# The rows of x2 by target: fetched through the first layer's packed list and a table, and the attention layer in two column parts

## The reference

```
h = max(layernorm(x), 0);  x = x + L0(h, src, dst)        # sums over edges, 1/sqrt(1 + degree)
h = max(layernorm(x), 0);  x = x + L1(h, [src, dst])      # polynomial of the graph Laplacian, 4 steps
h = max(layernorm(x), 0);  x = x + L2(h, src, dst, type)  # attention over edges, 86 relation types
h = max(layernorm(x), 0);  x = x + L3(h, src, dst)        # 10 steps of propagation, summed at dst
```

## Time and profile before

| | |
|---|---|
| median of three runs | 2741.11 us (2739.32 to 2743.00) |
| the profiled execution | 2739.09 us, span 2737.3 us |
| POOL busy | 1796.4 us (66%), 1786 instructions |
| DVE busy | 1731.8 us (63%), 2937 instructions |
| PE busy | 430.9 us (16%) |
| ACT busy | 341.8 us (12%) |
| granted TensorE clock | 1.0 |

### The profile page before, as it was taken

How to read it: one execution, slowest core, us unless ns; L and a number is a source line. 1 busy time by engine, 2 the same in 40 slices (tenths; PEclk the granted TensorE clock), 3 DMA queues, 4 the chain that set the end, 5 groups by cost and what they waited for, 6 DMA issues and landing times.

```text
span 2737.3 us, 12492 instructions
## 1 busy us (share of the span) xinstructions
PE 430.9 (16%) x2105; PEld 214.0 (8%) x2105; DVE 1731.8 (63%) x2937; ACT 341.8 (12%) x1043; POOL 1796.4 (66%) x1786
## 2 busy tenths in 40 slices
PE   0000000000001000000000097293294000016000
PEld 0000000000001000000000032031131000016000
DVE  8998897987129978278996078487888820420000
ACT  0000022111000110011211043141142200000000
POOL 6566677777742473577777656756556777466776
DMA  1001022221000131112210100100000210000000
GB/s 20 15 10 26 14 61 51 51 68 32 12 7 4 62 129 25 33 47 86 51 34 14 10 2 6 10 2 6 6 7 8 87 40 10 29 11 10 8 8 8
DMA packets 68011, 76.87 MB, mean 28 GB/s; under 512 B 34800, under 2 KB 60873, under 8 KB 67193
## 3 DMA queue, kind: packets, MB, share of 16 engines
q0 software_dynamic: 56384, 23.45, 6.5%
q1 hardware_dynamic: 5720, 27.38, 2.6%
q10 hardware_dynamic: 5856, 25.60, 2.5%
HBM read 35.67 MB, written 46.87 MB: 30 GB/s over the span
## 4 chain that ended last, share of the span: by engine, by line
DVE 45%; issue 27%; POOL 11%; PE 7%; another core or an unknown queue 5%; DMA 2%; ACT 1%; DVEq 1%; ACTq 0%; SPq 0%; POOLq 0%
POOL out L1573 9%; DVE mf L521 4%; DVE psum L903 3%; DVE psum L918 3%; DVE z L521 3%; DVE pay L521 2%; DVE outs L521 2%; PE psum L2017 2%; DVE pay L904 2%; PE psum L2018 2%; POOL mf L1567 1%; DVE psum L550 1%; DVE psum L913 1%; DVE xs L908 1%
## 5 line engine op out<-in xcount | busy, mean ns | idle before, releaser
L1567 POOL DMA_INDIRECT xs<-in_x,i_src x196 | 200.8, 1025 | 134.4 <-issue 56.4
L1567 POOL DMA_INDIRECT xd<-x_rows,i_dstX x196 | 195.9, 1000 | 128.5 <-DVE z L1377 93.9
L1567 POOL DMA_INDIRECT xd<-in_x,i_dst x196 | 205.1, 1046 | 109.3 <-DVE mf L521 47.5
L1573 POOL DMA_INDIRECT out<-outs,i_outS x196 | 200.7, 1024 | 112.7 <-issue 41.4
L1567 POOL DMA_INDIRECT mf<-x_rows,i_srcX x196 | 207.5, 1059 | 72.1 <-issue 72.1
L1573 POOL DMA_INDIRECT out<-outs,i_srcX x196 | 196.7, 1003 | 69.3 <-issue 58.9
L1567 POOL DMA_INDIRECT pay<-payload_by_dst,i_rank x196 | 195.2, 996 | 62.9 <-issue 62.9
L521 DVE TENSOR_TENSOR pay<-psum,pay 128x512 f32<-128x512 f32 x196 | 132.4, 688 | 117.5 <-ACT pay L1895 59.5
L521 DVE TENSOR_TENSOR mf<-mf 128x128 f32<-128x128 f32 (+5 forms) x578 | 175.7, 342 | 10.4
L2017 PE MATMUL psum<-pay 64*128 64x512 f16 x196 | 117.6, 600 | 183.6 <-ACT pay L1880 96.3
L1377 DVE TENSOR_REDUCE z<-pay 128x512 f32 (+1 forms) x196 | 132.4, 676 | 0.0
(11 more groups left out here) (458 smaller groups left out, 2398.4 us busy)
## 6 DMA issues: line engine op xcount, KB each, us to landing
z<-in_x ACTq DMA_DIRECT2D x14, 624.0 KB
out<-z ACTq DMA_DIRECT2D x14, 624.0 KB
l_first_rows<-mf SPq DMA_DIRECT2D x2, 3234.0 KB
outs<-in_x ACTq DMA_DIRECT2D x6, 624.0 KB
out<-outs ACTq DMA_DIRECT2D x6, 624.0 KB
l_own_rows<-pay SPq DMA_DIRECT2D x1, 3626.0 KB, 11.1
payload_by_dst<-z SPq DMA_DIRECT2D x1, 3234.0 KB
x_rows<-z SPq DMA_DIRECT2D x1, 3234.0 KB
```

What stands on the lines that cost most here:

```text
L1567: G.indirect_dma_start(out=dest(k), out_offset=None, in_=table, in_offset=bass.IndirectOffsetOnAxis(ap=idx[:, k:k + 1], axis=0), bounds_ch ...
L1573: G.indirect_dma_start(out=table, out_offset=bass.IndirectOffsetOnAxis(ap=idx[:, k:k + 1], axis=0), in_=source(k), in_offset=None, bounds_ ...
```

## The change

The target rows are no longer gathered one set of 128 for each of 196 columns. What `xd` holds before (the closed form for every edge) is stored by SP as a table `y_dram` in edge order, behind the store of x2. The listing of L1 packs a third value, the rank of the edge in target order (`rank_f`), so that each of the 128 x 46 list slots also knows the row of its edge (`dst_slot`). After L1, POOL gathers x2 for the list slots by `pf0` (46 columns, `PACKED`), then the source rows of part 0 (76), then scatters `PACKED` into the table by `dst_slot` (46), and SP loads the whole table back into `xd`; DVE waits for both transfers (`y_table`, 32) inside `l2_inputs`. If a list were longer than XW, the Else branch gathers all 196 columns as before.

The attention columns go in two parts, 0 to 76 and 76 to 196. The source rows of part 1 are all gathered during the first 18 turns, 50 columns free and then one for each finished column, so the listing of L3 follows the first 18 turns, and then inputs 1 (120 columns) and 31 turns. The sends are 40 beside the listing, 20 free, 124 beside the last turns.

```diff
-L2_PARTS = ((0, 76), (76, 140), (140, EC))
+L2_PARTS = ((0, 76), (76, EC))
 XS_PARTS = ((0, 66), (66, 140), (140, 180), (180, EC))
 OWN_PARTS = ((0, 140), (140, 180), (180, EC))
-L2_TURNS = ((0, 18), (18, 34), (34, EC // 4))
-ROWS_FREE = (0, 60, 50)
-SENDS_LISTING, SENDS_FREE, SENDS_BESIDE = 40, 20, 56
+L2_TURNS = ((0, 18), (18, EC // 4))
+ROWS_FREE = 50
+SENDS_LISTING, SENDS_FREE, SENDS_BESIDE = 40, 20, 124
...
-        g_at = 2 * HOT_N + 2 * CELL_N
-        EDGES = {"l1": edge_groups(two(out_t, 0, HOT_N), two(out_t, 2 * HOT_N, CELL_N), two(out_t, g_at, GIVEN_N)),
+        GIVEN3_N = XG * W * 3
+        EDGES = {"l1": edge_groups(two(out_t, 0, HOT_N), two(out_t, 2 * HOT_N, CELL_N), two(z_t, 0, GIVEN3_N), 3),
-                                   [out_t[:, late:late + GIVEN_N], xs_t[:, late:late + GIVEN_N]])}
-        assert g_at + 2 * GIVEN_N <= EW and x4c_at + 2 * HOT_N <= EC * OWNW
+                                   [out_t[:, late:late + GIVEN_N], xs_t[:, late:late + GIVEN_N]], 2)}
+        rank_f = z_t[:, 2 * GIVEN3_N:2 * GIVEN3_N + EC]
+        both_f = z_t[:, 2 * GIVEN3_N + EC:2 * GIVEN3_N + EC + 6 * W]
+        PACKED = pay[:, x4c_at:x4c_at + W * X2W].rearrange("p (q w) -> p q w", w=X2W)
...
             sp.wait_ge(s["s2_ready"], 1)
             sp.dma_start(x2_dram.rearrange("(p c) w -> p (c w)", p=P), z_t[:]).then_inc(s["s2_stored"], 16)
+            by_dst = y_dram.rearrange("(p c) w -> p (c w)", p=P)
+            sp.dma_start(by_dst, xd_t[:]).then_inc(s["y_table"], 16)
             sp.wait_ge(s["fits1_set"], 1)
             longest = sp.value_load(fits[0:1, 0:1], min_val=0, max_val=EC)
...
+                sp.wait_ge(s["y_scattered"], 16 * W)
+                sp.dma_start(xd_t[:], by_dst).then_inc(s["y_table"], 16)
...
             def keyed(ids, w, idx, cont, head, carried, away):
 
-                empty = c["st2"][:, 0:2 * w].rearrange("p (q v) -> p q v", v=2)
+                nv = len(idx)
+                empty = c["st2"][:, 0:nv * w].rearrange("p (q v) -> p q v", v=nv)
                 link(ts(empty, ids, 0.5, FAR, ALU.is_lt, ALU.mult))
                 link.many([V.scalar_tensor_tensor(out=out, in0=ids[:, :, k], scalar=-1.0, in1=empty[:, :, k],
...
-            def compact_edges(ptr, own, turned, edges):
+            def compact_edges(given, pointers, turned, edges, both):
...
-                for value, out in zip((ptr, own), values):
+                for value, out in zip(given, values):
...
+                nv = len(given)
+                ids = c["sq_out"][:, 0:nv * W].rearrange("p (q v) -> p q v", v=nv)
+                gathered_up(ids, W, nv, both)
+                keyed(ids, W, pointers, contc, headc, wc[:], nohome)
...
+            link(V.tensor_copy(rank_f, icols["edgeS"][:]))
             link(V.tensor_copy(icols["l1"][:], PAY[:, :, D]))
-            compact_edges(PAY[:, :, D], col("send"), wt, EDGES["l1"])
+            compact_edges((PAY[:, :, D], col("send"), rank_f), (pf0, owni, dst_slot[:]), wt, EDGES["l1"], both_f)
             segment_sums(link, PAY[:, :, 0:D], s["carry_in"], s["carry_out"], 1, None)
             marks["summed"] = link.n
...
                 halves_of(xy16[:, :, 0:D], xy16[:, :, D:2 * D], xy[:, :, D:2 * D])
-                dve.wait_ge(s[f"x2dst_in{part}"], 16 * w)
+                dve.wait_ge(s["y_table"], 32)
                 layernorm(xd, z, xy[:, :, D:2 * D], w=w)
...
             l2_turns(*L2_TURNS[0])
             pointers(1)
+            marks["ends"] = link.n
+            link(V.tensor_copy(icols["l3"][:], col("kn")))
+            compact_edges((col("kn"), col("own")), (pf0, owni), wt, EDGES["l3"], c["tmp"])
+            marks["ended"] = link.n
             l2_inputs(1)
             l2_turns(*L2_TURNS[1])
-            pointers(2)
-            marks["ends"] = link.n
-            link(V.tensor_copy(icols["l3"][:], col("kn")))
-            compact_edges(col("kn"), col("own"), wt, EDGES["l3"])
-            marks["ended"] = link.n
-            l2_inputs(2)
-            l2_turns(*L2_TURNS[2])
...
-            for part, (lo, hi) in enumerate(L2_PARTS):
-                ahead = 0
-                for dest, idx, landed in ((lambda k: XY[:, k, 0:X2W], "srcX", "x2src_in"), (lambda k: XDW[:, k, :], "dstX", "x2dst_in")):
-                    for k in range(lo, hi):
-                        if part > 0 and ahead >= ROWS_FREE[part]:
-                            done = min(4 * L2_TURNS[part - 1][0] + ahead - ROWS_FREE[part], 4 * L2_TURNS[part][0])
-                            pool.wait_ge(s["l2_done"], 2 + done)
-                        gather(dest, x2_dram, icols[idx], last[P * EC], s[f"{landed}{part}"], 1, k)
-                        ahead += 1
+
+            def x2_rows(part):
+                lo, hi = L2_PARTS[part]
+                for k in range(lo, hi):
+                    behind = k - L2_PARTS[1][0] - ROWS_FREE
+                    if behind > 0:
+                        pool.wait_ge(s["l2_done"], 2 + behind)
+                    gather(lambda q: XY[:, q, 0:X2W], x2_dram, icols["srcX"], last[P * EC], s[f"x2src_in{part}"], 1, k)
+
+            with pool.If(longest <= XW):
+                gather(lambda q: PACKED[:, q, :], x2_dram, pf0, last[P * EC], s["y_packed"], W)
+                x2_rows(0)
+                pool.wait_ge(s["y_table"], 16)
+                pool.wait_ge(s["y_packed"], 16 * W)
+                scatter(y_dram, lambda q: PACKED[:, q, :], dst_slot, last[P * EC], s["y_scattered"], W)
+            with pool.Else():
+                pool.wait_ge(s["y_table"], 16)
+                gather(lambda k: XDW[:, k, :], x2_dram, icols["dstX"], last[P * EC], s["y_packed"])
+                x2_rows(0)
+            x2_rows(1)
...
                     if k < SENDS_LISTING:
                         pool.wait_ge(s["dve"], min(marks["ends"] + 5 * (k + 1) // 2, marks["ended"]))
                     elif 0 <= beside < SENDS_BESIDE:
-                        pool.wait_ge(s["l2_done"], 2 + 4 * L2_TURNS[2][0] + beside)
+                        pool.wait_ge(s["l2_done"], 2 + 4 * L2_TURNS[1][0] + beside)
                     scatter(out, lambda q: OUT[:, q, :], icols["outS"], last[N], s["outs_scattered"], 1, k)
...
-            place_edges(0, 0, "l1")
+            place_edges(0, 0, "l1", 3)
...
-            split = L2_TURNS[2][0] // 2
+            split = L2_TURNS[1][0] // 2
             with pe.Fori(0, split) as i:
                 for half in range(2):
                     l2_turn(2 * i + half, half)
-            place_edges(8, XW // XG + 1, "l3")
+            place_edges(8, XW // XG + 1, "l3", 2)
```

More of the change, by code:

```diff
@@ L290, in build @@
         late = L2_PARTS[-1][0] * D
[L291 to L292 removed]
+        GIVEN3_N = XG * W * 3
+        EDGES = {"l1": edge_groups(two(out_t, 0, HOT_N), two(out_t, 2 * HOT_N, CELL_N), two(z_t, 0, GIVEN3_N), 3),
                  "l3": edge_groups(two(pay, x4c_at, HOT_N), two(z_t, late, CELL_N),
[L294 to L295 removed]
+                                   [out_t[:, late:late + GIVEN_N], xs_t[:, late:late + GIVEN_N]], 2)}
+        rank_f = z_t[:, 2 * GIVEN3_N:2 * GIVEN3_N + EC]
+        both_f = z_t[:, 2 * GIVEN3_N + EC:2 * GIVEN3_N + EC + 6 * W]
+        PACKED = pay[:, x4c_at:x4c_at + W * X2W].rearrange("p (q w) -> p q w", w=X2W)
+        assert 2 * GIVEN3_N + EC + 6 * W <= EW and x4c_at + W * X2W <= EC * OWNW
+        assert 2 * HOT_N + 2 * CELL_N <= EW and x4c_at + 2 * HOT_N <= EC * OWNW
         assert late + max(GIVEN_N, 2 * CELL_N) <= EW
@@ L343, in build @@
         SPREAD = ps[0][:, 512:1024]
-        PLACED = ps[0][:, 0:4 * W]
+        PLACED = ps[0][:, 0:6 * W]
         PAIRS = ps[1][:, 0:W3 * P]
@@ L491, in _ @@
                 sp.dma_start(x2_dram.rearrange("(p c) w -> p (c w)", p=P), z_t[:]).then_inc(s["s2_stored"], 16)
+                sp.wait_ge(s["y_packed"], 16 * EC)
+                sp.dma_start(by_dst, xd_t[:]).then_inc(s["y_table"], 16)
             listed_tables("l3", ((0, EC),))
@@ L1028, in _ @@
             placed = [0]
-            def compact_edges(ptr, own, turned, edges):
+            def compact_edges(given, pointers, turned, edges, both):
                 rev, act, code = c["tmp"][:, 0:EC], c["tmp2"][:, 0:EC], c["st1"]
                 vals, aux, valid = (c["st2"][:, k * XW:(k + 1) * XW] for k in range(3))
-                values = [c["sq_out"][:, k * XW:(k + 1) * XW] for k in range(2)]
+                values = [c["sq_out"][:, k * XW:(k + 1) * XW] for k in range(len(given))]
                 place, wide = c["sq_in"][:, 0:EC], c["tmp"][:, 0:P]
@@ L1037, in compact_edges @@
                 link(ts(rev, rev, float(EC), SPLIT, ALU.add, ALU.mult))
-                link(ts(act, ptr, FAR / 2, None, ALU.is_lt))
+                link(ts(act, given[0], FAR / 2, None, ALU.is_lt))
                 link(V.scalar_tensor_tensor(out=act, in0=lin, scalar=E - 0.5, in1=act, op0=ALU.is_lt, op1=ALU.mult))
                 link(V.tensor_tensor_scan(place, act, act, 0.0, ALU.add, ALU.max))
-                for value, out in zip((ptr, own), values):
```

(12 more changed lines are left out.)

15 lines of the change are left out of this document (7 added, 8 removed).

## The result

The changed kernel took 2700.11 us (median of 4 runs, 2696.4 to 2701.59) against 2741.97 for the kernel before on the same chip (4 runs, 2739.32 to 2743.0): ratio 0.9847, 95% interval 0.983 to 0.9864. Forecast were 2727 and -12 us; measured are -42, and between the two profiled spans 2737.3 - 2698.0 = 39.3. The direction was right; the forecast gain was less than a third of the measured one.

The account below looks back on a forecast made before the run. No engine alone was taken as the bound: DVE's listing before L1, slow turns beside POOL's flood, POOL behind the turns. Terms +54 +2 +0 -38 -30 = -12 took 2739.1 to 2727 us; 8-in-10 range 2688 to 2750.

Parts of the forecast that it names:

- A: L1's listing on DVE: third value 43.4 us at 1.40 a step, with wider work +54, all on the path; bounds -8, +57.
- R1: Rival for L1's listing: third value runs at L3's pace, 9.0 us not 43.4; total 2693, or 2665; chance 0.2.
- B: SP's store of the table behind x2's, +1 (bounds 0 and +11), and POOL's new If, +1: sum +2 us.
- C: First part, to the end of 18 turns: table 22 us late but recovered in the slow stretch: 0, bounds -8 and +22.
- D: Rest of the turns: 350 us for 389.0, 34 from the second slow stretch, 5 a missing input set; -38 us.
- E: POOL behind the turns: fewer sends left, so L3's own gather starts 70.5 us after them, not 100.9; gain 30.3.
- R2: Rival: slow stretch belongs to entering the loop of turns, not POOL's flood; 2749, up to 2783; chance 0.2.

Follow-up runs that it names:

- three_parts: Changed kernel with the column parts of before (76, 64, 56) and the listing back behind the second part: 2729.13 us beside 2691.3 for the changed kernel.
- flood_later_c: Changed kernel with POOL holding back part 1's source rows until 16 columns are through, on a chip with stretches: 2746.15 us (kernel before 2743.4).
- changed_c: The changed kernel run again, unaltered, on a chip without stretches: 2489.33 us against 2501.68 for the kernel before, ratio 0.9951.
- third_value_only: Kernel before with only the third value added to L1's listing, made and not used, on a chip without stretches: ratio 1.0003.

## Why the prediction was wrong

- **A, the step that failed.** I priced the third value at 43.4 us on top of everything else, "all on the path". The 1.40 us a step was right, the sum was not: the stretch ended where it had ended before, by POOL's flood and not by DVE's work, and 31 more steps in it push 30 others out of it, into fast time. +54 became +21.5: 13.2 us up to the first one-hot product (828.4 for 815.2, the 30 displaced steps in fast time), and 8.3 behind it, of which 6.7 are the wider products, as forecast. The 28 us that these 30 steps could save stood in my lower bound, as something for the case that the third value is fast too; it came true with a slow third value, 54 - 28 = 26. R1 had nearly the right size (2693) with a wrong mechanism: pacing POOL did not speed up the third value, the stretch ended 36 us after it. The row that I held against R1, 1.40 us from 771 to 813 beside a paced POOL, was that delay. The row that I held for it was misread: in L3's listing POOL's pace never bound, its sends went out back to back, and DVE's steps were fast all the same. I could have seen in the earlier trace rows that the rate changes at about 814, where nothing in DVE's work changes.
- **B** cost nothing: own rows +21.5, the packed gather +20.8.
- **C** was off by 10 us, for a mis-sized term. DVE waited 25.1 us for the table (forecast 22), and the lag from the flood's end to the fast columns was again 17 us (1584.6 to 1602). But the flood ended some 9 us later than I had it: 220 transfers took 292.4 us, 1.33 each, where I had 218 and used the 1.30 (and 1.28) of single rows. The flood of before says the same: 215 transfers from 1271.37 to 1557.9, 1.33 each. This gives most of the 10 us.
- **D** was right to the microsecond in its parts: pointers, listing and inputs 126.0 us (71 + 55), 31 turns 224.2. three_parts shows that 31.5 of the 34 us belong to the flood and not to the entry.
- **E** was right: 69.7 us for 70.5, POOL idle for 53.45 us, released by `l_own_rows`.
- **R2** fell with flood_later_c. On a chip without stretches its effect, not its cause, is there: the 18 turns end 33 us later (1565.13 in changed_c for 1531.73 in third_value_only), and in changed_c DVE then waits for POOL's last source rows.
- The section "Instruction fetch mechanics" of the Trainium skill's page "Runtime: NRT & Kernel Launch", by which instructions are fetched ahead and the fetch is hidden, fits the chips without stretches (111 DVE instructions from 660 to 700 us in changed_c) and not the others (31 from 680 to 720 before). No run shows whether it is the fetch that holds them.

## What to carry to other kernels

A slow rate is not a price per step until it is known what ends it: look for the point at which the rate changes, and ask whose work ends there. If it is another engine's, added steps displace others into fast time, and the sum is what they cost there. For the length of a flood divide its whole span by its count, not the gap of two rows. And where a gain comes from time in which every engine waits, measure on a second chip before calling it the kernel's. If an edit made of two parts is kept, undo one: here the part that looked like the idea, the table, gained nothing without the other.

## What the runs showed of the hardware

- One program, 2500 us on chips 9, 4 and 5 and 2728 to 2743 on chips 1 and 3 and that of the result. What the traces show of the difference lies in stretches beside and shortly behind POOL's long rows of back-to-back indirect transfers: short DVE steps start every 1.40 us, POOL's own issues lie 1.40 us apart in place of 1.30 (from 723.75 to 775.2 before), ACT takes up a finished product 13 us late.
- The granted clock of TensorE is 1.0, 2.4 GHz, through the kernel before and falls towards 0.5, 1.2 GHz, in the listing of every kernel with the third value, in the changed kernel from 843 us on, while PE works on the wider placing products (64 matmuls of 276 columns for 184). From 866 us it is 0.5 to the end. It cost nothing that shows: the 64x512 product took 631 ns in both kernels (its end is modelled, but the starts of two neighbouring ones lie 0.40 us apart in both as well), and 31 turns took the 224 us that the rows at 1.0 had promised. The page's groups, before and after:

```profile
L2018 PE MATMUL psum<-pay 64*128 64x512 f16 x196 | 123.6, 631 | 0.0
```

```profile
L2042 PE MATMUL psum<-pay 64*128 64x512 f16 x196 | 123.6, 631 | 0.0
```
